# Two gated MLPs and a projection stage of a fused two-block network: the rest tile on two column groups, and work moved between and within VectorE and ScalarE

## The reference, cut to what matters

```python
DIM = 256; HID = int(DIM * 4 * 2 / 3)          # 682
h = shift_token(x)                             # second half of the features comes from the token before
h = (h - mu) / jnp.sqrt(var + 1e-05) * lg + lb
h = h @ w1 + b1                                # 256 -> 2 * 682
a, g = jnp.split(h, 2, axis=-1)
h = a * jax.nn.gelu(g, approximate=False)
x = x + h @ w2 + b2                            # 682 -> 256
...
h = _layernorm(x, axis=-1) * (1 + ca) + sa     # second block
q, k, v = W_Q, W_K, W_V applied to h; q, k = _rope(q), _rope(k)
```

## Time and profile before

| | before |
|---|---|
| median of 3 runs | 4325.37 us |
| profiled execution: time, span | 4327.25 us, 4325.6 us |
| TensorE matmul busy | 3880.3 us (90%) |
| VectorE busy | 3372.1 us (78%) |
| ScalarE busy | 2553.8 us (59%) |
| GpSimd busy | 1169.8 us (27%) |
| MLP of layer 0, from its first to its last up or down product | 1309.9 to 1508.8 us |
| MLP of layer 1, likewise | 1969.1 to 2175.7 us |
| projections of the second attention | 2181.6 to 2295.9 us |

### The profile page before, as it was taken

One profiled execution on the slowest core, in us unless ns is written; L12 is line 12 of the kernel. 1 busy time (PEld: TensorE's weight loads), 2 busy tenths in 40 slices (PEclk: granted clock), 3 DMA queues, 4 the chain that ended last, 5 costly groups with the idle time before them and its releaser, 6 DMA issues. The chain is left out here.

```text
span 4325.6 us, 95192 instructions
## 1 busy us (share of the span) xinstructions
PE 3880.3 (90%) x38484; PEld 2197.5 (51%) x38484; DVE 3372.1 (78%) x5530; ACT 2553.8 (59%) x3441; POOL 1169.8 (27%) x958
## 2 busy tenths in 40 slices
PE   7999999669989969998986999999999999867996
PEld 4788888535555535555553332332333333434764
DVE  5688888779985479985787899999998978585454
ACT  3566666545554345653423777787888887635563
POOL 1122221277861067761141000000000000013552
PEclk9999999889999989999997999999999999977998
DMA  1011110133320033320063000000000000032444
GB/s 62 5 40 31 40 31 18 44 70 62 64 47 28 0 70 65 64 49 8 0 140 65 9 9 2 9 2 2 9 2 2 9 2 9 4 99 74 90 106 103
DMA packets 290198, 167.00 MB, mean 39 GB/s; under 512 B 204596, under 2 KB 281096, under 8 KB 289288
## 3 DMA queue, kind: packets, MB, share of 16 engines
q1 hardware_dynamic: 267176, 125.49, 13.5%
q0 software_dynamic: 13440, 21.24, 2.7%
q10 hardware_dynamic: 9184, 14.68, 1.1%
HBM read 77.81 MB, written 38.58 MB: 27 GB/s over the span
## 5 line engine op out<-in xcount | busy, mean ns | idle before, releaser
L2211 DVE TENSOR_REDUCE s_tops<-ps 128x2 f32<-128x1024 f32 (+3 forms) x1152 | 1250.2, 1131 | 143.4 <-PE ps L2097 104.0
L2180 ACT ACTIVATE s_weights<-ps 128x1024 f32<-128x1024 f32 (+3 forms) x1152 | 1092.7, 952 | 343.2 <-PE ps L2110 192.6
L2132 PE MATMUL ps<-s_weights,v_flat 128*32 128x256 f32 (+1 forms) x8704 | 692.8, 390 | 7.1 <-ACT s_o_t L2186 6.0
L2091 PE MATMUL ps<-keys,s_q 48*128 48x512 f16 (+3 forms) x2304 | 434.7, 375 | 48.1 <-DVE s_tops L2211 27.2
L2110 PE MATMUL ps<-s_q,keys 50*128 50x512 f16 (+3 forms) x2304 | 434.5, 374 | 45.9 <-DVE s_tops L2211 33.6
L2247 POOL CAST s_shift<-s_minus_top 128x16 f16<-128x16 f32 x32 | 6.3, 196 | 1428.2 <-DVE s_minus_top L2218 1428.2
L583 PE MATMUL ps<-a_qt,a_kt 128*128 128x256 f16 x3072 | 375.3, 273 | 3.8 <-POOL s_ones L538 3.8
L2110 PEld LDWEIGHTS ps<-s_q,keys 50*128 50x128 f16 x2304 | 112.2, 93 | 511.6 <-issue 252.5
L1173 PE MATMUL ps<-attention_w,la_yt 128*128 128x512 f16 x1152 | 289.9, 399 | 37.9 <-DMA la_yt<-la_y_parts 30.4
L583 PEld LDWEIGHTS ps<-a_qt,a_kt 128*128 128x128 f16 x3072 | 300.8, 98 | 40.3 <-POOL s_ones L538 4.2
L1248 ACT ACTIVATE la_weights<-ps 128x1024 f32<-128x1024 f32 x124 | 126.9, 1023 | 296.4 <-PE ps L1163 296.4
(11 more groups left out here) (371 smaller groups left out, 7209.4 us busy)
## 6 DMA issues: line engine op xcount, KB each, us to landing
ex_whole<-in_L_ffn_w_dram ACTq DMA_DIRECT2D x14, 1024.0 KB
qk_parts<-a_parts SPq DMA_DIRECT2D x64, 128.0 KB, 4.1
keys<-qk_parts SPq DMA_DIRECT2D x48, 128.0 KB, 5.2
s_q<-qk_parts SPq DMA_DIRECT2D x48, 128.0 KB, 4.8
x<-in_x_dram SPq DMA_DIRECT2D x8, 512.0 KB, 9.4
attention_w<-attention_split SPq DMA_DIRECT2D x2, 2048.0 KB, 9.0
la_table<-in_rotary_dram SPq DMA_DIRECT2D x64, 64.0 KB, 2.1
a_table<-in_rope_dram POOLq DMA_DIRECT2D x8, 512.0 KB, 5.7
```

The source lines that it names most:

```text
L2091: mm = pe.matmul(m.ps[:, bank, 0:width], b.q[rows(half, KEY_PARTS * L1_DH), place % 2, pair, t * P:(t + 1) * P], m.keys[rows(half, KEY_PAR ...
L2132: mm = pe.matmul(m.ps[h * QUAD:(h + 1) * QUAD, OUT, begin:end], m.v_flat[:, first:first + QUAD], weights[:, a % 2, h, begin:end], start=(k ...
L2180: act.activation(weights[:, a % 2, 2 * pair:2 * pair + 2, skip:CHUNK], m.ps[:, bank:end + 1, skip:CHUNK], ACT.Exp).then_inc(s["exp"], 1)
L2211: dve.tensor_reduce(tops[:, u % 2, :, i % 2, t, c], m.ps[:, bank:end + 1, 0:width], AX.X, ALU.max).then_inc(s["max"], 1)
```

## The change

1. In both MLPs the rest tile (42 units) of `up` runs as `up_rest`: g on output partitions 64 to 105, a on 0 to 41, with `tile_position` 0 and 64, and the matmuls of g and a alternate. Both waits stand ahead of both.
2. The low part of the rest tile of `hid` goes to partitions 64 to 105 of the high part's buffer, and w2's high rest rows are loaded at both places, so that `down` has 17 matmuls for a row tile instead of 18. w2 comes in four DMAs instead of one.
3. In both MLPs `norm` for chunk c+2 is cut into row tiles and runs inside `gate` of chunk c, after tiles 1, 2, 4 and 5. The wait for `next` (`back`) that stood ahead of `norm` now stands at the start of `gate`.
4. In layer 1 `weight`, `add` and `moments` move out of `gate` to between the pieces of `residual` (the last chunk still has them in its gate).
5. In the projections `norm` moves from VectorE to ScalarE, as scale and bias of an activation, between `high` of outputs 1 and 2.

```diff
-    sp.dma_start(b.b1[0:rest, n, MLP_TILES - 1:MLP_TILES], ...)
+    sp.dma_start(b.b1[n * REST_AT:n * REST_AT + rest, n, MLP_TILES - 1:MLP_TILES], ...)
...
+    NORMED_BY = {1: 0, 2: 1, 4: 2, 5: 3}
...
-                sp.dma_start(w2_flat[:, :, :], ...).then_inc(s["w2_in"], 16)
+                sp.dma_start(w2_flat[:, :, 0:full], w2_split[:, :, 0:full]).then_inc(s["w2_in"], 16)
+                sp.dma_start(w2_flat[:, 1, full:], w2_split[:, 1, full:]).then_inc(s["w2_in"], 16)
+                for to in (0, REST_AT):
+                    sp.dma_start(w2_flat[to:to + REST_AT, 0, full:], w2_split[0:REST_AT, 0, full:]).then_inc(s["w2_in"], 16)
...
                 def gate(c, u, between=None):
+                    if exists(c + 2):
+                        dve.wait_ge(s["back"], 32)
                     def low(e):
                         need(dve, s["hid_high"], ET * c + e + 1)
                         rows = slice(0, sizes[e])
-                        dve.scalar_tensor_tensor(hid[rows, u, 1, e, :], hid_whole[rows, e % 2, :], ...
+                        to = hid[low_rest, u, 0, e, :] if e == ET - 1 else hid[:, u, 1, e, :]
+                        dve.scalar_tensor_tensor(to, hid_whole[rows, e % 2, :], ...
...
                             ht_low(c + 1, 1 - u)
+                        elif e and e <= TPC + 1 and exists(c + 2):
+                            norm(c + 2, u, range(NORMED_BY[e], NORMED_BY[e] + 1))
...
-                def residual(c):
+                def residual(c, between=None):
                     for j in range(TPC):
...
+                        if between:
+                            between(j)
...
                     for c in range(CHUNKS):
-                        gate(c, c % 2, add_to_x(c - 1) if c else None)
+                        if c + 1 < CHUNKS:
+                            gate(c, c % 2)
+                            residual(c, add_to_x(c - 1) if c else None)
+                        else:
+                            gate(c, c % 2, add_to_x(c - 1))
+                            last_chunk(c)
...
-                        if exists(c + 2):
-                            dve.wait_ge(s["back"], 32)
-                            norm(c + 2, c % 2)
...
+                def up_rest(c, u, e):
+                    need(pe, s["gelu"], ET * c + e - 2 + 1)
+                    need(pe, s["hid_whole"], ET * c + e - 2 + 1)
+                    terms = [(k, p, q) for k in range(KD) for p, q in TERMS]
+                    for i, (k, p, q) in enumerate(terms):
+                        for part, made in ((1, s["g_mm"]), (0, s["a_mm"])):
+                            at = part * REST_AT
+                            mm = pe.matmul(m.ps[at:at + REST, 2 + 2 * (e % 2) + part, :], b.w1[...], ht[:, u, q, k, :],
+                                           start=(i == 0), stop=(i == len(terms) - 1), tile_position=(0, at), skip_group_check=True)
...
-                        terms = [(e, p, q) for e in range(ET) for p, q in TERMS]
+                        terms = [(e, p, q) for e in range(ET - 1) for p, q in TERMS] + [(ET - 1, 0, 0), (ET - 1, 0, 1)]
...
             @block.scalar    # attention1_projections
+                def norm(c, u):
+                    need(act, s["turned"], KD * (c - 1))
+                    for j in range(TPC):
+                        t = bass.ts(c * TPC + j, 1)
+                        n = act.activation(normed[:, u, j:j + 1, :], m.x[:, t, :], ACT.Identity, bias=minus[:, t], scale=m.rstd[:, t])
+                    n.then_inc(s["normed"], 1)
...
+                norm(0, 0)
+                norm(1, 1)
+                act.wait_ge(s["ones"], 1)
+                scaled(0, 0)
+                with act.Fori(0, CHUNKS // 2 - 1) as k:
+                    for u in range(2):
+                        scaled(k * 2 + u + 1, 1 - u)
+                        high(k * 2 + u, u, lambda: norm(k * 2 + u + 2, u))
```

More of the change, by code:

```diff
@@ L903 @@
 MLP_LOADS = 8
+REST_AT = P // 2
 def load_mlp(sp, m, b, a, layer, loaded):
@@ L1478, in _, with norm @@
                 credit(dve, s["normed"], s["ht"], s["hid_whole"], s["hid"], s["y"])
-                def norm(c, u):
+                def norm(c, u, rows=range(TPC)):
                     need(dve, s["turned"], KD * (c - 1))
-                    for j in range(TPC):
+                    for j in rows:
                         t = bass.ts(c * TPC + j, 1)
@@ L1498, in low @@
                         rows = slice(0, sizes[e])
-                        dve.scalar_tensor_tensor(hid[rows, u, 1, e, :], hid_whole[rows, e % 2, :], 1 / SCALE, hid[rows, u, 0, e, :],
+                        to = hid[low_rest, u, 0, e, :] if e == ET - 1 else hid[:, u, 1, e, :]
+                        dve.scalar_tensor_tensor(to, hid_whole[rows, e % 2, :], 1 / SCALE, hid[rows, u, 0, e, :],
                                                  ALU.mult, ALU.subtract).then_inc(s["hid"], 1)
@@ L1526, in add, with moments @@
                     dve.tensor_tensor(x, x, y, ALU.add).then_inc(s["x"], 1)
-                def moments(c, half):
+                def moments(c):
                     dve.wait_ge(s["x"], c + 1)
-                    for t in range(c * TPC + half * TPC // 2, c * TPC + (half + 1) * TPC // 2):
+                    for t in range(c * TPC, (c + 1) * TPC):
                         n = dve.bn_stats(m.six[:, t, :], m.x[:, t, :])
-                    if half:
-                        n.then_inc(x_sems["six"], 1)
+                    n.then_inc(x_sems["six"], 1)
                 def add_to_x(c):
@@ L1541, in piece @@
                             add(c)
-                        if e in (2, 4):
-                            moments(c, e // 4)
+                        if e == 2:
+                            moments(c)
                     return piece
@@ L1629, in gelus @@
                         rows = slice(0, sizes[e])
-                        act.activation(gelu[rows, e % 2, :], m.ps[rows, 3 + 2 * (e % 2), :], ACT.Gelu, bias=b.b1[rows, 1, e:e + 1],
+                        act.activation(gelu[rows, e % 2, :], m.ps[gate_rows(e), 3 + 2 * (e % 2), :], ACT.Gelu, bias=b.b1[gate_rows(e), 1, e:e + 1],
                                        scale=1 / SCALE).then_inc(s["gelu"], 1)
@@ L1806, in _ @@
             def _(dve):
-                credit(dve, s["normed"], s["rot"], s["low"])
-                def norm(c, u):
-                    need(dve, s["turned"], KD * (c - 1))
-                    for j in range(TPC):
-                        t = bass.ts(c * TPC + j, 1)
-                        n = dve.tensor_scalar(normed[:, u, j:j + 1, :], m.x[:, t, :], m.mean[:, t], m.rstd[:, t], ALU.subtract, ALU.mult)
-                    n.then_inc(s["normed"], 1)
+                credit(dve, s["rot"], s["low"])
+                dve.scalar_tensor_tensor(minus[:, :], m.mean[:, :], -1.0, m.rstd[:, :], ALU.mult, ALU.mult).then_inc(s["minus"], 1)
                 def rotate(c, u):
@@ L1851, in scaled, with high @@
                                        scale=m.modc[:, KD + k:KD + k + 1]).then_inc(s["ht"], 1)
-                def high(c, u):
+                def high(c, u, norm_ahead=None):
                     for n in range(OUTS):
+                        if norm_ahead and n == KD:
+                            norm_ahead()
                         need(act, s["sum"], OUTS * c + n + 1)
```

45 lines of the change are left out of this document (27 added, 18 removed).

## The result

The changed kernel takes 4302.31 us (median of 5 runs, 4300.86 to 4305.27) against 4325.37 us, a ratio of 0.995 with a 95% interval of 0.9938 to 0.9962. Measured once more it gave 4303.60 us and 0.995 (0.9936 to 0.9963). The forecast was 4302 us.

| | before | after | gain | forecast |
|---|---|---|---|---|
| MLP of layer 0 | 206.66 | 202.92 | 3.7 | 4.9 |
| MLP of layer 1 | 214.37 | 202.34 | 12.0 | 11.9 |
| projections | 124.04 | 117.38 | 6.7 | 6.8 |
| all that the change doesn't touch | | | 2.5 | 0 |

A forecast was written before the change was run, and what follows sets the result against it. TensorE was taken to bound layer 0, TensorE with a wait layer 1, VectorE the projections; gains of 4.9, 11.9 and 6.8, together 23.6 us, from 4325.4 gave 4302 us, range 4289 to 4316.

The forecast's parts named there:

- Matmuls, 1.73 a chunk: TensorE in both MLPs: 1.30 us less from overlapping column groups in the rest tile, 0.44 less in down, per chunk.
- Rival C: Rest tile of up: fp16 column groups run one after the other, so the kernel takes 4323 us; chance 0.08.
- The wait ahead of down, 0.9 to 1.0: End of a chunk: TensorE idles 0.9 to 1.0 us for VectorE's last low part, leaving 0.75 gain in layer 0's loop.
- Rival B: End of a chunk: chain shorter or only partly binding, 0.9 to 1.0 more saved in 13 chunks, 4290 us; chance 0.12.
- chunks of 22.8: Sign in layer 0's trace that TensorE's saving is kept whole; the forecast itself expected chunks of about 23.7 us.
- Layer 1, 11.9: MLP of layer 1: 11.9 us gained, 1.61 per loop chunk, of which 0.76 is its excess over layer 0.
- Start of layer 0, 1.8 lost: First chunk of layer 0: first hid_whole waits for the DMA into next, costing TensorE 1.8 us once.
- Layer 0, 3.7 instead of 4.9: MLP of layer 0: 4.9 us gained, as 6 x 0.75 + 1.2 + 1.0 - 1.8.
- Projections, 6.8: Projections: five norms leaving VectorE's loop save 6.8 us, with rotate chunks 12.2 us apart throughout.
- Rival D: Projections: ScalarE, or the stores high waits for, takes VectorE's place, nothing gained there, 4309 us; chance 0.10.
- Rival A: End of a chunk: GpSimd's bias gets ahead of the late low part, +30 us over twelve chunks, 4331 us; chance 0.10.

The follow-up runs named there:

- e4: Changed kernel, but only the last two products of down's first row tile wait for the rest tile's low part: 4283.58 us.
- e5: Changed kernel, but in the rest tile TensorE computes all six g products, waits for them, then computes the six of a: 4312.35 us.
- e3: Changed kernel with norm pieces after tiles 0, 1, 2 and 4, and GpSimd's bias also waiting for all low parts of the chunk: 4293.04 us.
- e9: Changed kernel, but in the MLPs only the column groups stay; norm is back behind the last residual, sums back in the gates: 4305.62 us.
- e8: Changed kernel, but layer 1's weight, add and sums of x are back inside the gates: 4302.18 us.
- e7: Changed kernel, but the second attention's projections are as before, with the norm on VectorE: 4308.51 us.
- e2: Changed kernel, but the four norm pieces stand after tiles 0, 1, 2 and 4, with no added wait for GpSimd's bias: 4313.52 us.

## Why the prediction was right

The chunks went as forecast, and the total came out closer than the parts, which is luck. The stages gained 22.4 instead of 23.6, the untouched rest of the profile happened to be 2.5 shorter, and the medians differ by 23.06. Of the 22.4, the clock of TensorE gave 0.75 in layer 1 and took 1.67 in layer 0 (below), and neither was in the sum.

- **Matmuls, 1.73 a chunk: right.** e4 shows it alone, 22.76. The overlap of fp16 products on two column groups, taken from f32 rows on four, holds, and e5 shows what is lost without it. Rival C is out. The Trainium skill, TensorEngine Tiling (Array Packing), Feature Incompatibilities, says that column tiling excludes the fast weight load. In this trace that costs nothing visible: the 12 rest products with their own loads take 1.41 us, not 2.3.
- **The wait ahead of down, 0.9 to 1.0: right**, 0.98 measured; net 0.74 a chunk in layer 0 against 0.75. As forecast, low stands behind the last norm piece, and that is about half of the wait: without it e3 and e9 have 0.53, which is the chain of the rest tile itself. Rival B would have needed a chain that doesn't bind; e4 is what it looks like when it doesn't, with the chunks of 22.8 that were named as its sign.
- **Layer 1, 11.9: right in size, partly by luck, and wrong in one reason.** The 0.76 went, but not because the sums left the gates (e8). It went with the norm's new place: with the old one, the column groups alone would leave 24.82 instead of 23.75 (e9). That the norm, cut up, lets the bias start late is the likely way, read from the rows. The 12.0 hides two misses. The five chunks of the loop gained 1.51 each and not 1.61, since down waits as long as in layer 0. The first chunk gained 1.50 and not 0.85: 0.75 of it is that its first 36 products, the same in both kernels, took 10.11 us instead of 10.86, at a granted clock of 0.78 over the first 10 us against 0.70. First the kernel before, then the changed one:

```profile
1969.07 10.86 PE L1661 MATMUL ps<-gm_ht,w 128*128 128x512 f16 x36 [2.87 <-DVE gm_ht L1493]
1966.56 10.11 PE L1693 MATMUL ps<-gm_ht,w 128*128 128x512 f16 x36 [2.87 <-DVE gm_ht L1508]
```

- **Start of layer 0, 1.8 lost: too much.** It was 1.28, the 0.54 by which the first chunk got longer and the 0.74 that it didn't gain:

```profile
1316.44 3.38 SPq L899 DMA_DIRECT2D next<-rows_own  x1
1321.33 1.41 DVE L1526 SCALAR_TENSOR_TENSOR gm_hid_whole<-ps,b_scaled,gm_gelu 128x512 f32<-128x512 f32 x2 [7.41 <-DMA next<-rows_own]
1322.14 1.47 PE L1693 MATMUL ps<-gm_ht,w 128*128 128x512 f16 x6 [1.24 <-DVE gm_hid_whole L1526]
```

  The mechanism is the forecast one. The issue took 3.38 where the earlier trace rows have 4.30, and hid_whole could start 8.38 behind the first up product, not 8.9.
- **Layer 0, 3.7 instead of 4.9.** 5 x 0.74 + 1.26 (chunk 6) - 0.54 (first chunk) + 0.53 (ups of the last) - 1.23 (last down 9.26 instead of 8.03) = 3.7. The last term is the mis-sized one: 0.44 of gain was forecast, and the clock took 1.67. In the second profile, where the last down ran at full clock, the layer takes 201.3, a gain of 5.4.
- **Projections, 6.8: right**, 6.7 there and confirmed by e7. Rival D is out; ScalarE's norm shows as 0.4 to 1.1 of wait on TensorE ahead of the transposes, and the rotates stay 12.2 apart all the same.
- **Rival A** did not come about, but by 0.16 us. e2 shows that GpSimd in front is real and costs 11 us; the 30 us priced for the other order were never run. The Trainium skill, SBUF — State Buffer, Who interferes with whom, describes an exclusive lock that goes to whoever issues first. The traces agree for both orders: first by 0.16, low keeps its 0.69 and the add takes 2.73; behind the add, the two low parts take 2.92 instead of 1.46.

## What to carry to other kernels

When a tile gets cheaper, look at which chain through other engines ends at its consumer: of 1.73 us saved, 0.98 was a new wait, and splitting one wait, so that only the products that read the late tile stand behind it, gave all of it back. Ask of each instruction that shares VectorE's and GpSimd's path not only how long it is but when it is released, and tie the long one behind the critical one by a semaphore rather than leave a margin of 0.16 us to the schedule. Undo the parts of a change one by one: here the norm by row tiles helped layer 1 and hurt layer 0, and moving the sums did nothing. And check a total that comes out right against its parts: here a clock that differed between two executions hid one miss and made another.

## What the runs showed of the hardware

- Products on different column groups need not alternate in the code: with all six of g first, the first of a started 0.453 us after g's first, and twelve took 1.86 us. Alternating takes 1.41, and 2.94 with a wait between.
- A GpSimd add of 128x1024 started 0.38 us ahead of a VectorE tensor_tensor of that size makes the latter 3.07 us instead of 1.22. A VectorE instruction that is first by 0.16 keeps its 0.69, and the add takes 2.73 instead of 2.36.
- After the same idle of 2.99 us the same 68 products took between 7.60 and 10.51 us: 7.60 at a granted clock of 1.00, 9.03 at 0.84 (e7, e9), 9.21 and 9.26 at 0.82, 10.51 at 0.71. What decides it is open.
